# A transformer feed-forward on one core: a padded last chunk, straight-line steps, a later turn of h, and two token tiles per z instruction

## What is computed

```python
x = x + 0.5 * ffn(layernorm(x))      # first feed-forward phase ("f1")
x = x + attention(layernorm(x))      # 16 heads of 16, softmax
x = x + 0.5 * ffn(layernorm(x))      # second feed-forward phase ("f2")

def ffn(x):                          # x: (4, 2048, 256) float32
    gate = fp4_linear(x, w_gate)     # 256 -> 704
    y = fp4_linear(x, w_up)          # 256 -> 704
    h = silu(gate) * y
    return fp4_linear(h, w_down)     # 704 -> 256

def fp4_linear(x, w):                # both operands are rounded to a 4-bit grid, in blocks of 16
    scale = max(max(abs(x_block)) / 6, 1e-12)
    xq = GRID[searchsorted(MID, abs(x / scale))] * sign(x) * scale    # GRID: 0 .5 1 1.5 2 3 4 6
    return einsum(xq, wq)
```

## Time and profile before

| | |
|---|---|
| median of 3 runs | 4297.5 us (4297.03 to 4298.36) |
| the profiled execution | 4299.67 us |
| its span, first to last instruction | 4297.8 us |
| first feed-forward phase, first to last matmul | about 74 to 654 us of the span |
| second feed-forward phase | about 3716 to 4294 us |
| PE busy | 4133.0 us, 96% |
| DVE / ACT / POOL busy | 3689.4 / 2471.5 / 1010.7 us |
| granted TensorE clock, mean | 0.983 |

### The profile page before, as it was taken

One profiled execution on the slowest core, in us unless ns is written; L12 is line 12 of the kernel. 1 busy time (PEld: TensorE's weight loads), 2 busy tenths in 40 slices (PEclk: granted clock), 3 DMA queues, 4 the chain that ended last, 5 costly groups with the idle time before them and its releaser, 6 DMA issues. The chain is left out here.

```text
span 4297.8 us, 113140 instructions
## 1 busy us (share of the span) xinstructions
PE 4133.0 (96%) x46770; PEld 2143.4 (50%) x46770; DVE 3689.4 (86%) x6452; ACT 2471.5 (58%) x2908; POOL 1010.7 (24%) x1188
## 2 busy tenths in 40 slices
PE   3999998979999999999999999999999999899999
PEld 2666665534444444444444444444444444666666
DVE  7888882669999999999999999999999994688887
ACT  1222224447777777777777777777777776222222
POOL 3777762310000000000000000000000001377776
PEclk7999999989999999999999999999999999999999
DMA  2000002310000000000000000000000000000000
GB/s 108 0 0 0 0 0 93 120 53 17 25 17 24 17 24 17 24 18 23 20 22 20 21 22 20 23 19 24 18 24 17 25 17 2 0 15 15 15 15 20
DMA packets 53335, 102.50 MB, mean 24 GB/s; under 512 B 10800, under 2 KB 37808, under 8 KB 52400
## 3 DMA queue, kind: packets, MB, share of 16 engines
q1 hardware_dynamic: 52912, 96.30, 6.6%
HBM read 61.93 MB, written 33.55 MB: 22 GB/s over the span
## 5 line engine op out<-in xcount | busy, mean ns | idle before, releaser
L871 DVE TENSOR_REDUCE mx<-ps_b 128x1 f32<-128x512 f32 x4032 | 2497.5, 683 | 108.6 <-PE ps_b L943 17.2
L858 ACT ACTIVATE probs<-ps_s 128x1024 f32<-128x1024 f32 x2048 | 1983.9, 1021 | 730.7 <-PE ps_s L990 730.7
L943 PE MATMUL ps_b<-K,Q 96*32 96x512 bf16 x16128 | 1597.1, 381 | 15.9 <-DMA K<-qk_parts_dram 14.5
L990 PE MATMUL ps_s<-Q,K 99*32 99x512 bf16 x16384 | 1430.7, 379 | 2.4 <-ACT probs L858 2.4
L968 PE MATMUL ps_o<-probs,V 128*32 128x512 f32 x8192 | 1062.8, 592 | 0.4 <-ACT probs L858 0.4
L990 PEld LDWEIGHTS ps_s<-Q,K 99*32 99x32 bf16 x16384 | 456.9, 97 | 622.7 <-issue 282.9
L943 PEld LDWEIGHTS ps_b<-K,Q 96*32 96x32 bf16 x16128 | 446.6, 96 | 637.9 <-issue 255.8
L489 PE MATMUL ps_gu_f<-w_guT,zT_f 128*128 128x352 f32 x2048 | 639.2, 466 | 7.1 <-DVE h_f L396 6.2
L489 PEld LDWEIGHTS ps_gu_f<-w_guT,zT_f 128*128 128x128 f32 x2048 | 386.0, 194 | 202.8 <-issue 9.8
L817 POOL TENSOR_TENSOR neg_parts<-neg_max,zeros 128x16 bf16<-128x16 f32 x64 | 14.1, 220 | 1893.4 <-issue 1793.2
L500 PE MATMUL ps_dn_f<-w_dnT,hT_f 128*128 128x256 f32 (+1 forms) x1536 | 379.3, 389 | 8.4 <-DVE x_res L384 6.6
(11 more groups left out here) (115 smaller groups left out, 2552.9 us busy)
## 6 DMA issues: line engine op xcount, KB each, us to landing
qk_parts_dram<-qk_parts SPq DMA_DIRECT2D x96, 256.0 KB, 2.8
Q<-qk_parts_dram SPq DMA_DIRECT2D x64, 192.0 KB
K<-qk_parts_dram SPq DMA_DIRECT2D x64, 192.0 KB
x_res<-in_L_attn_x SPq DMA_DIRECT2D x4, 2048.0 KB, 20.6
Q<-qk_parts_dram SPq DMA_DIRECT2D x64, 128.0 KB
K<-qk_parts_dram SPq DMA_DIRECT2D x64, 128.0 KB
out<-x_res SPq DMA_DIRECT2D x16, 512.0 KB, 2.6
Q<-qk_parts_dram SPq DMA_DIRECT2D x64, 64.0 KB
```

The source lines that it names most:

```text
L858: nc.scalar.activation(probs[:, (2 * kt + half) % 4, :], ps_s[:, half, :], ACT.Exp, scale=float(DH) ** -0.5).then_inc(exped, 1)
L871: nc.vector.tensor_reduce(mx[:, s, k // 4, bass.ds(k % 4, 1)], ps_b[:, bank, :], AX.X, ALU.max).then_inc(bank_free, 1)
L943: last = nc.tensor.matmul(ps_b[j:j + STRIP, bank, :], Q[s][0:PAIRS, qt * P + j:qt * P + j + STRIP], K[s][0:PAIRS, kb * 512:(kb + 1) * 512] ...
L990: last = nc.tensor.matmul(ps_s[j:j + STRIP, half, (c % 2) * 512:(c % 2 + 1) * 512], K[s][:, kt * P + j:kt * P + j + STRIP], Q[s][:, c * 51 ...
```

## The change

Four things are changed in `ffn_phase`, and one instruction is added to the weights phase.

1. *Straight.* `staged` gives way to `straight`, which writes every step out, so that each semaphore target is a constant.
2. *Padded.* The last chunk of h has 128 columns, of which 64 are zeros: `h_quant` is 768 wide, its end is set to zero once by POOL (PE waits for `pad_set`), and the unused 64 rows of the last chunk of `w_dnT` are set to zero by DVE at the program's start. Transposes, copy and products of that chunk have 128 rows, and ACT copies 768 columns by one instruction. So that this fits, `ps_hT` and `ps_zT` share two banks (`ps_T`: 768 + 256 columns). ACT therefore copies z only once PE has turned h of the same step, and PE turns z only once ACT has copied h of the step before. `ps_dn` has two banks instead of one.
3. *Later turning.* `LAG` is 3: PE turns h of tile i-3 in step i instead of i-2, and the down product, the copy and the addition to x follow.
4. *Two tiles per z instruction.* The z instructions of DVE and POOL are 512 wide, for the tiles of a `duo`. DVE issues its five, and POOL the first two (`z_scaled`, the addition), in even steps; POOL issues the other two in odd steps. ACT still normalises a tile per step, but for tile i+6.

```diff
@@ -222,6 +222,7 @@
 
                 W = W1 + W2
                 W0 = full * D
+                nc.vector.memset(m.w_dnT[LAST:P, FC - 1, :], 0.0)
                 dve.wait_ge(gate_loaded, 16)
...
-        ps_zT = bank("ps_zT", [P, 512])
-        ps_hT = bank("ps_hT", [P, 1024])
-        ps_dn = bank("ps_dn", [P, 512])
+        ps_T = bank("ps_T", [P, 1024])
+        ps_hT, ps_zT = ps_T[:, 0:FC * P], ps_T[:, FC * P:]
+        ps_dn = bank("ps_dn", [P, 2, 512])
...
-        stored = sem("stored")
+        stored, pad_set = sem("stored"), sem("pad_set")
+        AHEAD, LAG = 6, 3
...
+        def straight(step):
+            for i in range(-AHEAD, NT + LAG + 1):
+                step(i, i % 2, lambda k, i=i: 0 <= i + k < NT)
...
                     if live(1):
                         act.wait_ge(zT_turned, i + 2)
+                        if live(-LAG):
+                            act.wait_ge(hT_turned, i - LAG + 1)
                         if live(-1):
                             act.wait_ge(gu_done, i)
-                        nc.scalar.copy(zT[:, 1 - q, :], ps_zT[:, 0:KD * P]).then_inc(zT_kept, 1)
-                    if live(-2):
-                        act.wait_ge(hT_turned, i - 1)
-                        if live(-4):
-                            act.wait_ge(dn_done, i - 3)
-                        nc.scalar.copy(hT[:, q, 0:(FC - 1) * P], ps_hT[:, 0:(FC - 1) * P])
-                        nc.scalar.copy(hT[0:LAST, q, (FC - 1) * P:], ps_hT[0:LAST, (FC - 1) * P:FC * P]).then_inc(hT_kept, 1)
-                    if live(4):
-                        if live(2):
-                            act.wait_ge(z_scaled, i + 3)
-                        nc.scalar.activation(z[:, q, :], m.x[:, i + 4, :], ACT.Identity,
-                                             bias=m.shift[:, bass.ds(i + 4, 1)], scale=m.rstd[:, bass.ds(i + 4, 1)]).then_inc(z_ready, 1)
+                        nc.scalar.copy(zT[:, 1 - q, :], ps_zT).then_inc(zT_kept, 1)
+                    if live(-LAG):
+                        act.wait_ge(hT_turned, i - LAG + 1)
+                        if live(-LAG - 2):
+                            act.wait_ge(dn_done, i - LAG - 1)
+                        nc.scalar.copy(hT[:, 1 - q, :], ps_hT[:, 0:FC * P]).then_inc(hT_kept, 1)
+                    if live(6):
+                        t, duo = i + 6, (i + 6) // 2
+                        if duo >= 2:
+                            act.wait_ge(z_scaled, duo - 1)
+                        nc.scalar.activation(z[:, duo % 2, q * D:(q + 1) * D], m.x[:, t, :], ACT.Identity,
+                                             bias=m.shift[:, bass.ds(t, 1)], scale=m.rstd[:, bass.ds(t, 1)]).then_inc(z_ready, 1)
...
-                    here, z3, old = live(0), live(3), live(-3)
+                    here, z3, old = live(0), q == 0 and live(4), live(-LAG - 1)
+                    duo = (i + 4) // 2
+                    e = duo % 2
...
                     if z3:
-                        dve.wait_ge(z_ready, i + 4)
-                        nc.vector.tensor_reduce(zamax[:], blocks_of(z[:, 1 - q, :]), AX.X, ALU.max, apply_absolute_value=True).then_inc(z_step, 1)
+                        dve.wait_ge(z_ready, 2 * duo + 2)
+                        nc.vector.tensor_reduce(zamax[:], blocks_of(z[:, e, :]), AX.X, ALU.max, apply_absolute_value=True).then_inc(z_step, 1)
                     if old:
-                        dve.wait_ge(dn_done, i - 2)
-                        nc.vector.scalar_tensor_tensor(out=m.x[:, i - 3, :], in0=ps_dn[:, 0:D], scalar=0.5 / SHRINK**2,
-                                                       in1=m.x[:, i - 3, :], op0=ALU.mult, op1=ALU.add).then_inc(x_done, 1)
+                        dve.wait_ge(dn_done, i - LAG)
+                        nc.vector.scalar_tensor_tensor(out=m.x[:, i - LAG - 1, :], in0=ps_dn[:, q, 0:D], scalar=0.5 / SHRINK**2,
+                                                       in1=m.x[:, i - LAG - 1, :], op0=ALU.mult, op1=ALU.add).then_inc(x_done, 1)
...
+                        if duo >= 2:
+                            dve.wait_ge(pool_z, (duo - 1) * PZ_STEPS)
+                        nc.vector.tensor_scalar(zscale[:, e, :], zamax[:], SHRINK / 6.0, TINY, ALU.mult, ALU.max).then_inc(z_step, 1)
...
                     if z3:
-                        dve.wait_ge(z_scaled, i + 4)
-                        if live(2):
-                            dve.wait_ge(pool_z, (i + 2) * PZ_STEPS + 2)
-                        nc.vector.tensor_scalar(zM[:].bitcast(I32), zs[:, 1 - q, :].bitcast(I32), EXPONENT, None, ALU.bitwise_and).then_inc(m_step, 1)
+                        dve.wait_ge(z_scaled, duo + 1)
+                        if duo >= 1:
+                            dve.wait_ge(pool_z, (duo - 1) * PZ_STEPS + 2)
+                        nc.vector.tensor_scalar(zM[:].bitcast(I32), zs[:, e, :].bitcast(I32), EXPONENT, None, ALU.bitwise_and).then_inc(m_step, 1)
...
-                    if live(3):
-                        pool.wait_ge(z_step, (i + 4) * Z_STEPS)
-                        nc.gpsimd.tensor_tensor(blocks_of(zs[:, 1 - q, :]), blocks_of(z[:, 1 - q, :]), spread(zinv[:, 1 - q, :], D), ALU.mult).then_inc(z_scaled, 1)
-
-                        pool.wait_ge(m_step, (i + 4) * M_STEPS)
-                        nc.gpsimd.tensor_tensor(zr[:], zs[:, 1 - q, :], zM[:], ALU.add).then_inc(pool_z, 1)
-                        pool.wait_ge(pool_z, (i + 3) * PZ_STEPS + 1)
+                    duo = (i + 4) // 2
+                    e = duo % 2
+                    if q == 0 and live(4):
+                        pool.wait_ge(z_step, (duo + 1) * Z_STEPS)
+                        nc.gpsimd.tensor_tensor(blocks_of(zs[:, e, :]), blocks_of(z[:, e, :]), spread(zinv[:, e, :], 2 * D), ALU.mult).then_inc(z_scaled, 1)
+                        pool.wait_ge(m_step, (duo + 1) * M_STEPS)
+                        if duo >= 1:
+                            pool.wait_ge(pool_z, duo * PZ_STEPS)
+                        nc.gpsimd.tensor_tensor(zr[:], zs[:, e, :], zM[:], ALU.add).then_inc(pool_z, 1)
+                    if q == 1 and live(3):
+                        pool.wait_ge(pool_z, duo * PZ_STEPS + 1)
                         nc.gpsimd.tensor_tensor(zr[:], zr[:], zM[:], ALU.subtract).then_inc(pool_z, 1)
-                        pool.wait_ge(pool_z, (i + 3) * PZ_STEPS + 2)
-                        if live(1):
-                            pool.wait_ge(zT_turned, i + 2)
-                        nc.gpsimd.tensor_tensor(blocks_of(zq[:, 1 - q, :]), blocks_of(zr[:]), spread(zscale[:, 1 - q, :], D), ALU.mult).then_inc(pool_z, 1)
+                        pool.wait_ge(pool_z, duo * PZ_STEPS + 2)
+                        if duo >= 2:
+                            pool.wait_ge(zT_turned, 2 * (duo - 1))
+                        nc.gpsimd.tensor_tensor(blocks_of(zq[:, e, :]), blocks_of(zr[:]), spread(zscale[:, e, :], 2 * D), ALU.mult).then_inc(pool_z, 1)
                     if live(0):
                         pool.wait_ge(h_step, (i + 1) * H_STEPS)
                         if live(-1):
@@ -454,31 +469,34 @@
                         pool.wait_ge(hr_ready, i + 1)
                         if live(-2):
                             pool.wait_ge(hT_turned, i - 1)
-                        nc.gpsimd.tensor_tensor(blocks_of(hq[:, q, :]), blocks_of(hr[:]), spread(hscale[:, q, :], I), ALU.mult).then_inc(hq_ready, 1)
-
-                staged(pool, step, NT, 4, 4)
+                        nc.gpsimd.tensor_tensor(blocks_of(hq[:, q, 0:I]), blocks_of(hr[:]), spread(hscale[:, q, :], I), ALU.mult).then_inc(hq_ready, 1)
+
+                nc.gpsimd.memset(hq[:, :, I:], 0.0).then_inc(pad_set, 1)
+                straight(step)
...
                 def turn_z(i, q, live):
-                    pe.wait_ge(pool_z, (i + 2) * PZ_STEPS)
+                    duo = (i + 1) // 2
+                    pe.wait_ge(pool_z, (duo + 1) * PZ_STEPS)
                     if live(0):
                         pe.wait_ge(zT_kept, i + 1)
+                    if live(-LAG - 1):
+                        pe.wait_ge(hT_kept, i - LAG)
                     for k in range(KD):
-                        last = nc.tensor.transpose(ps_zT[:, k * P:(k + 1) * P], zq[:, 1 - q, k * P:(k + 1) * P], m.ident[:])
+                        last = nc.tensor.transpose(ps_zT[:, k * P:(k + 1) * P], zq[:, duo % 2, (1 - q) * D + k * P:(1 - q) * D + (k + 1) * P], m.ident[:])
                     last.then_inc(zT_turned, 1)
...
-                    if live(-2):
-                        pe.wait_ge(hq_ready, i - 1)
-                        if live(-3):
-                            pe.wait_ge(hT_kept, i - 2)
+                    if live(-LAG):
+                        pe.wait_ge(hq_ready, i - LAG + 1)
+                        if live(-LAG - 1):
+                            pe.wait_ge(hT_kept, i - LAG)
                         for c in range(FC):
-                            rows = P if c < FC - 1 else LAST
```

(16 more changed lines are left out.)

30 lines of the change are left out of this document (14 added, 16 removed).

## The result

| | before | after |
|---|---|---|
| median | 4297.26 us | 4263.68 us (4261.28 to 4266.97) |
| profiled execution / its span | 4299.67 / 4297.8 | 4261.28 / 4259.5 |
| DVE busy, whole span | 3689.4 | 3812.4 |
| POOL busy | 1010.7 | 922.7 |

The ratio is 0.9922, with a 95% interval of 0.9905 to 0.9939. The change gains 33.6 us, where 67.6 were forecast; 4263.7 lies above the range of 4221 to 4250. (The profiled execution is one of the lower ones; against that of before it is 38.4 us less.)

What follows compares the result with a forecast made beforehand. PE was taken to set the pace at 8.79 us per tile, to become 8.20. Steady part -69.1, start -0.7 and end +2.2 gave -67.6 us, so 4230 us, range 4221 to 4250.

Steps and rivals of the forecast that it cites:

- Straight: In the loop: register rows go, and with them the rest of the 0.25 us per tile.
- Padded: Down product and first transpose, 128 rows everywhere: saves PE 0.34 us per tile, bounds 0 and 0.34.
- Later turning: Turn of h: POOL gets one more tile, 8.2 us, for `h_quant`, so PE's present wait of at most 0.3 us goes.
- the 0.25 per tile: PE's loss in the loop alone, 8.79 - 8.54: 0.14 waiting for `h_quant`, 0.11 put down to refill and register work.
- Two tiles per instruction: z work of DVE and POOL: their time falls a little, nothing for PE in the steady part, a slower start.
- 69.1: Steady part, gate-and-up of tile 3 to tile 63: gain of 34.9 us in the first phase plus 34.2 in the second.
- B: Uneven DVE holds PE: even step has up to 8.81 us of work in 8.20; 4248 us (4238 to 4262), chance 0.17.
- D: POOL becomes the bound, stretched beside DVE's work; slower than before once a pair needs 17.5 us; chance 0.03.
- Start and end: Per phase: start about -0.35 us, end +1.1; for both phases -0.7 and +2.2.
- the 3.1 in front: Start of a phase: first gate-and-up 3.1 us later, from two activations (0.5), wider POOL (2.0) and DVE (0.6) instructions.

## Why the prediction was wrong

- *Padded, later turning, straight: right in what they do to PE.* The down product takes 2.59, as forecast, and where nothing else holds PE a tile takes 8.20. The waits for `h_quant` and "issue" at the 64-row records are gone. Straight with the later turn gave 35 us, of which 27.7 lie in the steady parts, where the 0.25 per tile make 30. What the prediction had wrong is "So PE sets the pace, at 8.79 us per tile": in the loop padding alone, which spares PE 0.34 us a tile, is worth nothing that can be told, because `h_quant` comes no sooner. It pays only together with the straight form and the later turn; that of the two it is the later turn is argued from that wait, and not tried. In this change all came together, so that this did not show in the total.
- *Two tiles per instruction: this step failed.* It said: "DVE's and POOL's time falls a little; neither sets the pace, so this gives PE nothing in the steady part." POOL's time fell (12.82 to 11.44 per pair), DVE's rose (14.37 to 16.62), and a pair took 17.07 instead of 16.40. From gate-and-up 3 to 63 it is 614.66 - 104.38 = 510.28 us in the first phase and 4235.14 - 3724.57 = 510.57 in the second, against 526.70 and 526.04 in the earlier trace rows: a gain of 31.9 where 69.1 were summed. The missing 37.2 us are more than the whole error of 33.7; starts and the stretch between the phases gave some of it back. That DVE waits for POOL here is shown: the wait goes away with narrow POOL instructions, and for the two scale instructions with the maxima in PSUM, while DVE's instructions stay as wide.
- *Where it could have been seen.* I costed DVE by busy time, and contention by one row of POOL (1.26 against 0.72). The rows of DVE before hold a 44-element instruction of 522 ns. The Trainium skill says it outright, on a page that the prediction did not weigh: "SBUF — State Buffer", section "SBUF: two separate sides", has VectorE and GpSimd share one pair of ports by an exclusive lock, held for the whole instruction, with the loser fully blocked. The 1.18 us that end 0.04 after POOL's instruction agree. By "VectorE: DVE Perf Modes", section "What auto-detection actually checks", a two-port mode wants, besides conditions on the shape, the single source and the destination in SBUF; the 204 ns with a source in PSUM agree.
- *The rivals.* B had the signature (8.2 and 8.5, PE waiting for `h`; measured 8.27 and 8.80) and nearly the time (4238 to 4262), with a wrong cause: 0.15 to 0.5 us per pair from length, where it was 0.67 from waiting. 4263.7 lies just above B's bounds. D had the cause, contention, but looked for it on POOL. I priced the two apart and did not see that contention would stretch DVE into B.
- *Start and end.* The first gate-and-up came 1.8 us later instead of 3.1 (75.76 against 73.94), tile 3's 1.9 earlier (0.35 forecast). Between the two the kernel is 3.7 us shorter in the first phase and 3.3 in the second, where 3.5 were forecast; in the start, the 3.1 in front was mis-sized. The end, from the last gate-and-up to the end of the last addition, is 4255.87 + 0.42 - 4235.14 = 21.15, forecast 21.0. From tile 63 of the first phase to tile 3 of the second it is 5.8 us less, where 0.75 more was forecast. The part of it up to the second phase's first gate-and-up took 3081 to 3084 us in the kernels with one-tile instructions and 3081 to 3090 in those with two, most of it attention, which no edit touches; what spreads it was not tried. The prediction also took the lower clock at both starts from the earlier trace rows. That row shows it in its first and ninth slice only, and the ninth, 860 to 967 us, is no feed-forward phase. A window of the kernel before has it at the second start: 0.78 over 3716 to 3728 us.
